# GpSimd instead of VectorE makes the low parts of the layer-0 weight slices of groups 1 to 15

## What is computed

```python
# layer 0: a weight matrix per category
x = x + einsum('bsd,bdh->bsh', x, W0[cat]) + b0[cat]
# layer 1: shared up projection, shared down projection, expert part of the output
h = gelu(einsum('bnd,hd->bnh', x, fc1_w) + fc1_b)            # 2048 columns
shared = einsum('bnh,sh->bns', h, fc2_w) + fc2_b             # 384 columns
expert = einsum('bnh,bph->bnp', h, We[exp]) + be[exp]        # 128 columns
x = x + concatenate([shared, expert], axis=-1)
```

## Time and profile before

| | |
|---|---|
| median of 3 runs | 1606.64 us |
| profiled execution, its own time | 1607.92 us |
| its span, first to last instruction | 1606.1 us |
| PE (TensorE matmul) busy | 1595.9 us, 99% |
| DVE (VectorE) busy | 1312.3 us, 82% |
| ACT (ScalarE) busy | 554.1 us, 35% |
| POOL (GpSimd) busy | 0.9 us, 8 instructions |
| granted TensorE clock | 1.0 of full speed |

### The profile page before, as it was taken

How to read it: one execution, slowest core, us unless ns; L and a number is a source line. 1 busy time by engine, 2 the same in 40 slices (tenths; PEclk the granted TensorE clock), 3 DMA queues, 4 the chain that set the end, 5 groups by cost and what they waited for, 6 DMA issues and landing times.

```text
span 1606.1 us, 27973 instructions
## 1 busy us (share of the span) xinstructions
PE 1595.9 (99%) x7102; PEld 1321.9 (82%) x7102; DVE 1312.3 (82%) x2189; ACT 554.1 (35%) x923; POOL 0.9 (0%) x8
## 2 busy tenths in 40 slices
PE   9999999999999999999999999999999999999999
PEld 7778888888888888888888888888888888888887
DVE  6878878888888888878888798887888888888765
ACT  5433333333333333333333333333333333333321
POOL 0000000000000000000000000000000000000000
PEclk9999999999999999999999999999999999999999
DMA  8765555545455455644555555555554555554420
GB/s 258 209 176 162 146 151 165 159 146 151 139 172 159 141 156 150 171 141 152 149 153 159 147 161 152 150 150 142 171 156 147 149 151 168 147 156 143 133 53 27
DMA packets 303474, 243.69 MB, mean 152 GB/s; under 512 B 34324, under 2 KB 235156, under 8 KB 303380
## 3 DMA queue, kind: packets, MB, share of 16 engines
q1 hardware_dynamic: 256404, 205.44, 45.2%
q10 hardware_dynamic: 46976, 37.38, 7.6%
HBM read 210.18 MB, written 32.51 MB: 151 GB/s over the span
## 4 chain that ended last, share of the span: by engine, by line
PE 92%; DMA 1%; DVE 0%; issue 0%; DVEq 0%; ACT 0%; ACTq 0%
PE ps_out L936 41%; PE ps_h L904 21%; PE ps_e L904 20%; PE ps_y L896 10%; DMA prep_raw<-in_L_cond_fc_w 1%; DVE resid L748 0%; PE ps_t L840 0%; DVE y L689 0%; DVEq L59 0%; DVE x_raw L696 0%; ACT g_raw L578 0%; ACTq L548 0%; ACTq L179 0%
## 5 line engine op out<-in xcount | busy, mean ns | idle before, releaser
L936 PE MATMUL ps_out<-w2e,h 128*128 128x512 f32 x3072 | 736.7, 389 | 0.0
L936 PEld LDWEIGHTS ps_out<-w2e,h 128*128 128x128 f32 x3072 | 576.0, 188 | 119.1
L904 PE MATMUL ps_e<-y_t,w 128*128 128x512 f32 (+1 forms) x1548 | 370.6, 388 | 0.0
L904 PE MATMUL ps_h<-y_t,w 128*128 128x512 f32 (+1 forms) x1548 | 370.2, 388 | 0.0
L904 PEld LDWEIGHTS ps_e<-y_t,w 128*128 128x128 f32 x1548 | 289.6, 188 | 59.8 <-DVE y_t L654 0.2
L904 PEld LDWEIGHTS ps_h<-y_t,w 128*128 128x128 f32 x1548 | 289.5, 188 | 59.2
L717 DVE STREAM_TRANSPOSE e_whole<-e_blocks 128x512 f32<-128x512 f32 x256 | 277.1, 1082 | 0.0
L564 ACT CAST w2e<-e_whole 128x512 fp32r<-128x512 f32 x256 | 158.6, 620 | 330.4 <-DVE e_whole L717 330.4
L736 DVE CAST h<-g_raw 128x512 fp32r<-128x512 f32 x256 | 108.7, 424 | 182.0 <-ACT g_raw L578 180.4
L532 ACT CAST w_split<-w_raw 128x512 fp32r<-128x512 f32 x244 | 146.6, 620 | 236.7 <-DMA w_raw<-in_L_cond_W 122.2
L654 DVE TENSOR_TENSOR w_split<-w_raw,w_split 128x512 fp32r<-128x512 f32 x244 | 159.3, 681 | 42.1 <-ACT w_split L532 40.9
(11 more groups left out here) (93 smaller groups left out, 411.7 us busy)
## 6 DMA issues: line engine op xcount, KB each, us to landing
e_blocks<-in_L_cond_experts_w SPq DMA_DIRECT2D x1024, 64.0 KB, 2.6
w_raw<-in_L_cond_W SPq DMA_DIRECT2D x248, 256.0 KB, 4.0
out<-resid SPq DMA_DIRECT2D x64, 256.0 KB, 2.2
x_blocks<-in_x SPq DMA_DIRECT2D x240, 64.0 KB, 2.8
b_all<-in_L_cond_b SPq DMA_DIRECT2D x60, 256.0 KB, 4.2
x_raw<-in_x SPq DMA_DIRECT2D x60, 256.0 KB, 4.8
y_rows<-y ACTq DMA_DIRECT2D x60, 256.0 KB, 4.2
x_blocks<-y_rows ACTq DMA_DIRECT2D x240, 64.0 KB, 2.3
```

The source lines that it names most:

```text
L904: last = nc.tensor.matmul(h_bank(c)[:, at * S:end * S], w1[:, w, k, c * P:(c + 1) * P], y_t[:, a, k, at:end, :].rearrange("p b s -> p (b s)"),
L936: last = nc.tensor.matmul(ps_out[b][:, :], h[:, c % 2, a, b * S:(b + 1) * S], fc2_columns(c, c % 2, w, b), start=(c == 0 and n == 0), stop ...
```

## The change

The two `w_low` at the head of VectorE's steps go. GpSimd has a loop of its own over the groups, in which it makes all 16 low parts of the next group one after another, each as soon as its high part is counted on `w_hi`. The low parts of the first group's slices stay with VectorE. Waits, semaphores, tiles and all other engines' instructions are the same.

```diff
@@ gpsimd @@
                 .then_inc(category_no_ready, 1)
 
 
+            def w_low(G, j):
+                after(pool, w_hi, w_lows(G, j))
+                nc.gpsimd.tensor_tensor(split_slot(G, j)[:, 1, :], w_slot(G, j), split_slot(G, j)[:, 0, :].bitcast(F32),
+                                        ALU.subtract).then_inc(w_lo, 1)
+
+            def body(g, more):
+                if more:
+                    for j in range(NC):
+                        w_low(g + 1, j)
+
+            groups(pool, body)
+
+
         @block.scalar
@@ vector @@
             def body(g, more):
                 for c in range(NC):
                     if more:
-                        for j in slices_in(c):
-                            w_low(g + 1, j)
                         for b in begun_in(c):
                             x_low(g + 1, b)
```

## The result

The changed kernel took 1610.67 us (median of 20 runs), the kernel before 1607.03 us (20 runs on the same chips): a ratio of 1.0021, 95% interval 1.0015 to 1.0027. It is slower by about 3.4 us, where no difference was forecast. All ratios here are of fast runs, which leaves out one execution of a later variant (2297.58 us).

What follows compares the result with a forecast made beforehand. TensorE was taken as the bound, gapless from 122 us on, so only the first group could move: -0.1 us on the profiled 1607.92, forecast 1606.5 us against the median, range 1604.2 to 1611; within 0.2% given 0.79.

Steps and rivals of the forecast that it cites:

- GpSimd's price: Each slice's low part on GpSimd: 1.2 us taken, bounds 0.68 and 2.3 us.
- The steady state costs nothing: Groups 1 to 15: GpSimd's low parts come in time, 3.4 us to spare in step 12, cost 0.
- Rival 2: Low slices become the bound: at 3.0 us per slice 24 us slower, 1630.6 us; chance 0.06.
- The sum over the first group: Replay of four TensorE gaps with mutual blocking: -0.1 us; without any disturbance -1.9 us.
- the gap at 99.73: First group: GpSimd holds up VectorE 1.2 us at 94.12, as much as the removal spares: 0.
- rival 1: First group: VectorE held up more than spared, about +7 us, 1613.6; decides from about 1.7 us per slice; chance 0.10.
- the four gaps: First-group TensorE waits with slices ahead of them, at 45.62, 55.06, 99.73 and 115.81: 3.2 us together.
- The gap at 55.06: First group: GpSimd works on the late second slice until 53.8, delaying the experts' low part from 53.30: +0.5 us.
- The smaller gaps: First group: the gap at 45.62 was to change by -0.4 us, that at 115.81 by -0.2 us.
- The gap at 121.00: End of the first group: a 0.4 us wait that belongs to a transfer and stays.
- VectorE's relief: Whole run: VectorE's busy time down from 1312.3 to about 1155 us, or its subtractions and fast copies longer where blocked.
- SP's wait for low parts: Whole run: SP's wait of 308.7 us before loading slices was to become smaller.

Runs made afterwards that it cites:

- Doubling the work: GpSimd makes the low parts of groups 2 to 15, each twice in a row, group 1's staying on VectorE: ratio 1.0481.
- GpSimd for groups 2 to 15: Changed kernel, but VectorE keeps the low parts of group 1's slices: ratio 1.0007 to the kernel before.
- the two with an unrelated instruction: Kernel before, plus a GpSimd subtraction or fill of 512 columns sharing no data, beside slice copies of groups 3 to 16: 1617.03 and 1606.57 us.
- GpSimd for group 1 alone: GpSimd makes only the low parts of group 1's slices, VectorE those of all later groups: ratio 1.0028 to before.
- bias adds moved: Changed kernel with the first group's output bias adds put into steps 3, 6, 7, 7: ratio 1.0014, median 1609.19 us.
- TensorE kept at work: Changed kernel with eight extra unused matmuls of 512 columns in step 3 of the first group: ratio 1.0021.
- The two kernels with slices 2 and 3 issued early: Slices 2 and 3 loaded ahead of biases, first bias adds a step later; on the changed kernel 1.0002 (1608.72 us), on the one before 0.9994 (1607.51).

## Why the prediction was wrong

- **What bounds the kernel, and where it could move: right.** TensorE is gapless from 122 to 1500 us with and without the change, and the whole difference in time came from the first group. A difference of 0.2% was called about what a measurement can tell; with 20 runs each the interval is 0.06% either way, and 0.2% is clear of it.
- **GpSimd's price: right.** 1.2 us was taken; one that meets nothing on VectorE takes 1.29 us, and the mean is 1.52, since it too waits up to 0.5 us for an instruction of VectorE. The upper end of 2.3 us was not reached.
- **The steady state costs nothing: right.** Doubling the work gave 1.0481, so the room was real and finite. Rival 2's price was too low there, since it counted 30 late steps and there were 98.
- **The sum over the first group failed**, -0.1 us forecast. Its term for the gap at 99.73, "what it holds up (1.2 us at 94.12) is what the removal gives back: 0", counted one meeting. There were two, one per bias add, 2.2 us lost against 1.2 spared: +1.00 us instead of 0. I had written "each of the four chains meets GpSimd twice" under rival 1, and did not replay the cautious end that way.
- **The list of gaps was too short.** I replayed the four gaps that the trace showed. Step 5 had the same order and the same bias adds, but no gap and no replay; it had no room either. TensorE waits 0.86 us there now, and is 1.00 us later behind it.
- **The gap at 55.06**: +0.5 was forecast for the blocking and it is +0.23, the gap itself 1.27 us larger. When slice 3 lands moves it by more than the blocking does. In six profiles with group 1's low parts on VectorE (before twice, GpSimd for groups 2 to 15, the same doubled, and the two with an unrelated instruction) the copy of slice 3 starts at 50.1 to 52.3 us, in six with them on GpSimd (the changed kernel three times, GpSimd for group 1 alone, bias adds moved, TensorE kept at work) at 50.8 to 53.9. The means are 1.2 us apart, but the ranges overlap, and six against six do not settle that the change makes the landing later. A way for it is that ScalarE's load of the next prepared tile is issued earlier, since the gap at 45 us is shorter (46.03 instead of 46.39), and its transfer comes among those of slice 3. That is argued, not shown: it wasn't tried alone.
- **The clock was not priced.** The lower level after the longer standstill took 1.6 us in the profiled execution. It is absent from some.
- **The smaller gaps went as forecast**: 0.77 to 0.43 us at 45, and that at 115.81 gone. The gap at 121.00, which was to stay, is gone too, but also in the second profile of before, so it is not the change's.
- **VectorE's relief** was forecast at 157 us or longer instructions. It was the second: 19 us. SP's wait for low parts (331.1 us in 189 waits against 308.7 in 84) did not shrink as I wrote; SP comes to the loads earlier as well.

What repeats: +1.00 and +1.00 for the bias adds in steps 5 and 9, -0.36 and -0.34 to -0.44 for the gaps that shrank, together 1.2 to 1.3 us. The two kernels with slices 2 and 3 issued early, which have no gap in step 3, are 1.2 us apart. The rest of the 3.4 us is step 3's gap and the slow stretch behind it, which differ from one execution to the next: 1.27 + 1.63 us in the first pair of profiles (1611.88 and 1607.92), 1.7 and 0 in the third of the changed kernel against the second of before (1608.69 and 1606.14). Parts that have nothing to do with the change come on top, -0.6 us in the first pair (the transfer's gap) and -0.9 in the other (TensorE's start, ahead of step 2). That they go with the first group is shown by GpSimd for group 1 alone, and that early loads of slices 2 and 3 end them by the run that did so; why the copy starts later with the change stays open. What happened is rival 1, with 1.5 us per slice where it was said to decide from 1.7; it had 0.10. The median stayed inside the range, which reached up to 1611 to take in part of that rival, but the forecast itself, no difference, was wrong.

## What to carry to other kernels

Moving work from VectorE to GpSimd relieves VectorE only where their instructions don't both need the shared way into SBUF: count each meeting at up to GpSimd's full duration (1.29 us for 512 columns; the bias adds lost 1.1 us each, the 163 lengthened instructions 0.76 on average), for every short instruction of VectorE that may stand there, a bias add of 0.28 us as well. When TensorE is the bound, look at the start-up, where it is not: replay every step of it that has the moved order, also those that show no gap, and put what TensorE waits for in front. And before a median's difference is explained by a mechanism, profile the same kernel again, since the landing of one transfer closed a gap of 1.4 us in one kernel and made it 1.5 or 3.0 us in the other.

## What had not been expected

- VectorE's blocked instructions took up to GpSimd's whole duration longer: 1.38 instead of 0.28 us, 1.52 instead of 0.42.
- A fill of 512 columns on GpSimd (0.52 us) lengthens VectorE's fast copies and not its subtractions.
- TensorE ran 9 matmuls in 3.00 us at a granted clock of 0.52 after standing still for 2.64 us amid a full load, and in another run after 1.86 us.
- Each low part made twice cost 78 us: a wait of about 0.7 us in seven of every eight steps with slices, not only in those that follow another.
